# Values held back one step and taken in pairs: a two-layer transformer kernel on one core

## The reference

```
xn = layernorm(x)
x  = x + diff_attention(xn; 16 heads, two softmax maps each) + (fp6_quantised(xn) @ fp6_quantised(W).T + bias)
xn = layernorm(x)
x  = x + rope_attention(xn; 16 heads, one softmax map each) + mlp(xn; sign weights, 128 -> 512 -> 512 -> 128, relu)
```

## Time and profile before

| | us |
|---|---|
| median of 3 runs | 860.47 |
| the profiled execution: its own time | 859.55 |
| its span, first to last instruction | 857.8 |
| PE busy | 801.4 (93%) |
| ACT busy | 764.2 (89%) |
| DVE busy | 551.5 (64%) |
| POOL busy | 35.4 (4%) |

### The profile page before, as it was taken

The page is one execution under the profiler, slowest core; times in us unless marked ns, Lnnn a source line. Parts: engine busy times, 40 slices in busy tenths (PEclk is TensorE's granted clock), DMA queues, the critical chain, the costliest instruction groups (busy, mean ns, idle before and its releaser), DMA issues.

```text
span 857.8 us, 17781 instructions
## 1 busy us (share of the span) xinstructions
PE 801.4 (93%) x6735; PEld 283.6 (33%) x6735; DVE 551.5 (64%) x1216; ACT 764.2 (89%) x856; POOL 35.4 (4%) x56
## 2 busy tenths in 40 slices
...
GB/s 110 166 119 123 53 91 135 124 57 50 164 50 148 7 106 108 107 97 2 164 50 141 64 1 213 50 126 30 51 164 89 115 2 151 53 2 139 75 13 13
DMA packets 42114, 75.52 MB, mean 88 GB/s; under 512 B 5920, under 2 KB 7584, under 8 KB 42016
## 3 DMA queue, kind: packets, MB, share of 16 engines
...
HBM read 36.84 MB, written 35.65 MB: 85 GB/s over the span
## 4 chain that ended last, share of the span: by engine, by line
PE 70%; ACT 12%; DVE 9%; issue 5%; DMA 2%; SPq 1%; DVEq 0%; ACTq 0%
PE ps_pv L899 30%; PE ps_s L880 20%; ACT probs L726 12%; PE ps_misc L747 7%; PE ps_misc L751 7%; PE ps_misc L752 5%; PE ps_misc L740 2%; DMA q_ab<-shift 1%; DMA parts_dram<-qk_parts 1%; DVE pv_sb L1346 1%; DVE v_aug L1205 0%; DVE h_lo L1139 0%; ACT ff_out L676 0%; SPq L457 0%; DVE h_hi L1137 0%
## 5 line engine op out<-in xcount | busy, mean ns | idle before, releaser
L726 ACT ACTIVATE probs<-ps_s 128x1024 f32<-128x1024 f32 x768 | 725.8, 1048 | 54.8 <-PE ps_s L880 53.7
L899 PE MATMUL ps_pv<-probs,v_aug 128*32 128x512 f32 x3072 | 412.0, 608 | 8.6 <-ACT probs L726 4.6
L880 PE MATMUL ps_s<-q_ab,k_ab 18*128 18x512 f32 (+1 forms) x1088 | 142.6, 497 | 29.9 <-ACT probs L726 23.9
L880 PEld LDWEIGHTS ps_s<-q_ab,k_ab 18*128 18x128 f32 (+1 forms) x1088 | 54.6, 183 | 204.1 <-ACT probs L726 164.1
L899 PEld LDWEIGHTS ps_pv<-probs,v_aug 128*32 128x32 f32 x3072 | 61.7, 108 | 116.2 <-issue 82.8
L751 PE MATMUL ps_misc<-h_hi,k_w 128*128 128x512 f32 x192 | 85.8, 447 | 2.4 <-DVE v_aug L1205 1.2
L880 PE MATMUL ps_s<-q_c,k_c 34*128 34x512 f32 x448 | 84.1, 451 | 0.0
L1137 DVE CAST h_hi<-ff_out 128x512 fp32r<-128x512 f32 x64 | 27.4, 427 | 86.9 <-ACT ff_out L676 85.1
L1346 DVE STREAM_TRANSPOSE pv_sb<-ps_pv 128x512 f32<-128x512 f32 x48 | 34.4, 717 | 74.6 <-PE ps_pv L899 72.0
L752 PE MATMUL ps_misc<-h_lo,k_w 128*128 128x512 f32 x192 | 75.9, 395 | 0.0
L751 PEld LDWEIGHTS ps_misc<-h_hi,k_w 128*128 128x128 f32 x192 | 35.9, 187 | 88.9 <-issue 50.4
...
## 6 DMA issues: line engine op xcount, KB each, us to landing
...
parts_dram<-qk_parts SPq DMA_DIRECT2D x62, 256.0 KB, 4.0
...
x_all<-in_L_attn_x_dram POOLq DMA_DIRECT2D x7, 256.0 KB, 4.2
out_dram<-x_all POOLq DMA_DIRECT2D x7, 256.0 KB, 7.1
```

Source lines behind the costliest of these rows:

```text
L726: nc.scalar.activation(probs[:, U.slot(s), 2 * half:2 * half + 2], ps_s[:, 2 * pair:2 * pair + 2], ACT.Exp, scale=SCALE[U.layer]).then_inc ...
L880: ins = nc.tensor.matmul(ps_s[:, bank, :], k[row:row + n, slot, c * P:(c + 1) * P], q[row:row + n, slot, :], start=True, stop=True)
L899: ins = nc.tensor.matmul(ps_pv[32 * j:32 * j + 32, :], v_aug[:, U.v, c, a:a + 32], probs[:, U.slot(s), j, :], start=c == 0 and not odd, st ...
```

## The change

1. A step may be marked with an item `hold`. In a held step S, PE makes the scores and the jobs but not the values of S-2; in step S+1 the values of S-2 and S-1 come one behind the other, and then the jobs of S+1. The order of the values is worked out by `order_of_values`. A third number in a `hold` item has no effect.
2. `probs` has a fourth slot, so the exponentials of S wait for the values of S-4 only.
3. x is kept in a ring of four (`x_ring`), which makes room for the fourth slot. POOL loads sequences 2 and 3 where it loaded all, and sequence b+2 behind `x_t1` of b, once sequence b-2 is stored. The parked v goes to slot 0 of the ring.
4. The tables: 21 of the 48 steps of a turn of the loop are held, seven in each stage. Single steps are held in `FIRST` (2) and `LAST` (8). In `LOOP`, jobs move: `project1` and one half of `ff1` stay in A, three parts of `ff1` and `ff1_b` that were in A and the first steps of B are spread over B, and `quant_mm`, the last part of `ff1` and `ff1_b`, `ff2` and `ff2_b` come to stage C. `v1` moves from step 9 of A to step 8, and `qk_norm1` stays in step 9, but ahead of `take`. `exact0` moves from B to step 7 of C.

```diff
+RING = 4
+SLOTS = 4
@@
 LOOP = [
-    {0: [("ff0", -1, 0)], 1: [("take", -2, "C", 1), ("ff0", -1, 1)], 2: [("regroup", -2, "C", 1)], 3: [("q1", -1)],
+    {0: [("hold", 0, 0), ("ff0", -1, 0)], 1: [("take", -2, "C", 1), ("ff0", -1, 1)], 2: [("regroup", -2, "C", 1)],
...
-     7: [("rope", -1, "k", 0), ("rope", -1, "k", 1)], 9: [("v1", -1), ("take", 0, "A", 0), ("qk_norm1", -1)], 10: [("ff0", -1, 3)],
+     8: [("hold", 0, 8), ("v1", -1)], 9: [("qk_norm1", -1), ("take", 0, "A", 0)], 10: [("hold", 0, 10), ("ff0", -1, 3)],
...
+def order_of_values():
+
+    order, due = [], []
+    for S in range(STEPS * UNITS):
+        due += [S - 2] if S >= 2 else []
+        held = any(item[0] == "hold" for item in TABLE[S // STEPS].get(S % STEPS, []))
+
+        assert not held or (S % 8 != 1 and len(due) == 1), S
+        order.append([] if held else due)
+        due = due if held else []
+    return order, [*due, STEPS * UNITS - 2, STEPS * UNITS - 1]
@@
     def slot(self, s):
-        return (self.first_step + s) % 3
+        return (self.first_step + s) % SLOTS
@@
-        probs = sb("probs", [P, 3, 4, N], F32)
+        probs = sb("probs", [P, SLOTS, 4, N], F32)
@@
+            load_x(1, x1_loaded)
+            pool.wait_ge(scores_made, 2 * STEPS)
+            for b in range(2, RING):
+                load_x(b, x_loaded)
@@
+            def load_next(b):
+
+                if RING <= b < NSEQ:
+                    pool.wait_ge(stored, 16 * (b - RING + 1))
+                    load_x(b, x_loaded)
@@
-                        wait(act, pv_made, S - 2)
+                        wait(act, pv_made, S - SLOTS + 1)
@@
-                    if s >= 2:
-                        pv(U, s - 2)
-                    elif u > 0:
-                        pv(Unit(u - 1), STEPS - 2 + s)
+                    for earlier in order[STEPS * u + s]:
+                        pv(Unit(earlier // STEPS), earlier % STEPS)
                     run(items, holds)
```

More of the change, by code:

```diff
@@ L79 @@
      12: [("norm0", 1, 1), ("bias", 0), ("quant_mm", 0)], 14: [("norm0", 1, 2), ("norm0", 1, 3)], 15: [("norm0", 1, 4), ("x_t0", 1)]},
[L80 to L83, removed]
+    {0: [("q0", 1)], 1: [("take", 0, "A", 1)], 2: [("lambda", 0), ("regroup", 0, "A", 1)], 3: [("quant", 1, 0), ("v0", 1)],
+     4: [("quant", 1, 1), ("quant", 1, 2)], 5: [("k0", 1)], 6: [("quant", 1, 3)], 7: [("quant", 1, 4)], 9: [("exact0", 1)],
+     10: [("take", 0, "B", 0), ("regroup", 0, "B", 0)], 11: [("quant", 1, 5), ("quant", 1, 6)], 12: [("bias", 1)],
+     13: [("quant_mm", 1)]},
     {1: [("take", 0, "B", 1), ("regroup", 0, "B", 1), ("combine", 0, 0)], 3: [("combine", 0, 1), ("combine", 0, 2)],
@@ L103 @@
 LOOP = [
[7 rows of a table removed]
[L111 to L117, removed]
[7 rows of a table added]
+     3: [("quant", 1, 0)], 4: [("hold", 0, 20), ("ff1", -1, 1), ("quant", 1, 1)], 5: [("quant", 1, 2)],
+     6: [("hold", 0, 22), ("ff1_b", -1, 1)], 7: [("quant", 1, 3)], 8: [("hold", 0, 24), ("q0", 1)],
+     9: [("take", 0, "B", 0), ("quant", 1, 4)], 10: [("hold", 0, 26), ("ff1", -1, 2), ("quant", 1, 5)],
+     11: [("regroup", 0, "B", 0), ("quant", 1, 6)], 12: [("hold", 0, 28), ("ff1_b", -1, 2)], 13: [("bias", 1)], 14: [("k0", 1)]},
+    {0: [("hold", 0, 32), ("ff1", -1, 3)], 1: [("take", 0, "B", 1), ("regroup", 0, "B", 1), ("ff1_b", -1, 3)],
+     2: [("hold", 0, 34), ("quant_mm", 1), ("combine", 0, 0)], 3: [("combine", 0, 1), ("combine", 0, 2)],
+     4: [("combine", 0, 3), ("combine", 0, 4)], 5: [("combine", 0, 5)], 6: [("hold", 0, 38), ("v0", 1), ("out_t0", 0)],
[3 rows of a table added]
+     14: [("hold", 0, 46), ("ff_t", -1)]},
 ]
 LAST = [
[5 rows of a table removed]
[6 rows of a table added]
     {0: [("ff1", 5, 2), ("norm0", 7, 3)], 1: [("take", 6, "A", 1), ("norm0", 7, 4), ("ff1_b", 5, 2)],
@@ L128 @@
      4: [("q0", 7), ("quant", 7, 2), ("quant", 7, 3), ("quant", 7, 4), ("quant", 7, 5)], 6: [("ff1", 5, 3)],
-     7: [("ff1_b", 5, 3), ("k0", 7)], 8: [("bias", 7)], 10: [("quant", 7, 6)], 11: [("take", 6, "B", 0), ("regroup", 6, "B", 0)],
-     12: [("exact0", 7), ("v0", 7)], 14: [("ff2", 5)]},
-    {0: [("ff2_b", 5)], 1: [("take", 6, "B", 1)], 2: [("regroup", 6, "B", 1), ("v_move", 5), ("combine", 6, 0)],
+     7: [("ff1_b", 5, 3), ("k0", 7)], 8: [("bias", 7), ("hold", 0, 24)], 10: [("quant", 7, 6)],
+     11: [("take", 6, "B", 0), ("regroup", 6, "B", 0)], 12: [("exact0", 7), ("v0", 7)], 14: [("ff2", 5), ("hold", 0, 30)]},
+    {0: [("ff2_b", 5), ("hold", 0, 32)], 1: [("take", 6, "B", 1)], 2: [("regroup", 6, "B", 1), ("v_move", 5), ("combine", 6, 0)],
      3: [("combine", 6, 1), ("combine", 6, 2), ("ff_t", 5)], 4: [("combine", 6, 3), ("quant_mm", 7)],
@@ L1198, in job @@
                 elif name == "v1" and b in (5, 6):
-                    dve.wait_ge(stored, 16 * finished[0])
-                    taken(nc.vector.tensor_copy(x_all[:, b - 5].rearrange("p t d -> p (t d)"), ps))
+                    assert finished[0] == 5
+                    dve.wait_ge(stored, 16 * 5)
+                    wait(dve, v_moved, b - 5)
+                    taken(nc.vector.tensor_copy(waiting_values.rearrange("p t d -> p (t d)"), ps))
                 elif name in ("v0", "v1"):
```

46 lines of the change are left out of this document (24 added, 22 removed), and 36 rows, old and new, of tables (FIRST, LAST, LOOP).

## The result

The changed kernel takes 866.05 us (median of 13 runs, 862.2 to 869.16) against 860.45 of the kernel before (13 runs beside them, 858.54 to 864.66): a ratio of 1.0061, 95% interval 1.0044 to 1.0077. It is slower by 5.6 us, where I forecast 858.0, and lies outside the range of 850.5 to 865. Its profiled execution took 864.89, 5.3 more than that of before, so the two profiles can stand for the medians.

What follows compares the result with a forecast made beforehand. Whether PE brings ACT's scores in time bounds A and B; C is near both engines' limits. Loop -1.6, held steps outside -0.9 and +0.2 make -2.3: 859.55 becomes 857.2, median 858.1, written 858.0; range 850.5 to 865.

Steps and rivals of the forecast that it cites:

- A: First stage of a loop turn: PE's steps sum to 34.3 us against 36.8 before, -2.5.
- B: Second stage of a loop turn: PE's steps sum to 32.3 us against 34.6 before, -2.3.
- C: Third stage of a loop turn: jobs moved in are paid in full, 34.7 us against 30.3 before, +4.4.
- pairs: In A and B, a held step of 1.68 and the step behind it of 2.31 take 3.99 us.
- the second values: On PE, values directly behind values take 0.88 us, with bounds of 0.86 and 0.99.
- The wait for `take`: In step 11 of A, PE waits 0.8 us because take has gone behind the norm chain; bounds nothing to 1.5.
- Rival 1: C runs late: a DVE chain starting 1.5 us late delays PE, 6 over four turns, 864; chance 0.23.
- rival 4: Values behind values gain nothing on PE: a pair takes 4.10 us, 9 more over four turns, 867; chance 0.03.
- The first and last stages keep their order but for ten held steps: Outside the loop: about eight held steps save 0.11 us each, -0.9; first values held one step cost 0.2.
- -0.4 a turn, -1.6 over four: The loop: changes of -2.5, -2.3 and +4.4 us in A, B and C sum to this gain.
- The ring costs nothing: x loads: each lands in 4.2 us and is issued some 90 us ahead of the norm that reads it.
- project1 of b = 4 moves to step 6: Outside the loop: it comes four steps (8 us) ahead of the v that needs its store.

Runs made afterwards that it cites:

- e1: The changed kernel without its ten held steps outside the loop, those in the loop kept: 863.19 us, ratio 1.0045 to the kernel before.
- e2: The changed kernel with the loop's table of the kernel before, the ten held steps outside the loop kept: 865.18 us, ratio 1.0062 to the kernel before.
- e3: The changed kernel with no held step and the old loop table; ring, fourth slot and jobs moved outside the loop stay: 862.39 us, ratio 1.0036.
- f3: e1 with stage A rearranged (take before qk_norm1, ff0's last part a step later, step 4 not held): 860.04 us, ratio 0.9987 to the kernel before.
- f1: The changed kernel with useless identity transposes in PE's longest idle times outside the loop: 861.56 us, ratio 1.0008 to the kernel before.
- g2: The changed kernel without three held steps beside long waits (step 2 of stage 0, 14 of 18, 0 of 19): 865.3 us, ratio 1.006.

## Why the prediction was wrong

**What held.** A was 34.2 for 34.3, B 32.3 for 32.3, C 34.7 for 34.7. Held steps are 1.68 and pairs in B without a relu 3.97 to 4.01, for 3.99. PE in B, answering to the earlier trace rows, shows a held step with its half of `ff1` (333.76 to 335.44; the job starts 0.43 behind the scores) and the pair behind it (335.88 to 337.77, 1.89 where two separate values would take 1.98):

```profile
333.76 0.50 PE L918 MATMUL ps_s<-q_ab,k_ab 18*128 18x512 f32 x4
334.19 0.51 PE L789 MATMUL ps_misc<-h_hi,k_w 128*128 128x512 f32 x1
...
335.44 0.51 PE L918 MATMUL ps_s<-q_ab,k_ab 18*128 18x512 f32 x4
335.88 1.92 PE L937 MATMUL ps_pv<-probs,v_aug 128*32 128x512 f32 x16
337.77 0.51 PE L918 MATMUL ps_s<-q_ab,k_ab 18*128 18x512 f32 x4
```

So the second values cost 0.90 in this pair (1.89 less 0.99). In the pairs of C they come to 0.86 or 0.87 (395.00 to 396.86 is 1.86), the lower end of the range; I had taken 0.88. A job behind scores starts after 0.43 to 0.44 in A and B, as taken. C answers to the earlier trace rows; PE is busy 34.58 of its 34.73:

```profile
394.25 0.83 PE L918 MATMUL ps_s<-q_c,k_c 34*128 34x512 f32 x4
395.00 1.92 PE L937 MATMUL ps_pv<-probs,v_aug 128*32 128x512 f32 x16
396.86 0.73 PE L918 MATMUL ps_s<-q_c,k_c 34*128 34x512 f32 x4
```

The wait for `take` came where and as large as forecast: 0.8. PE and DVE in step 11 of A, answering to the earlier trace rows:

```profile
321.16 0.68 DVE L1247 TENSOR_REDUCE norm_max<-ps_misc 64x1 f32<-64x512 f32 x1 [0.80 <-PE ps_misc L836]
...
322.73 0.50 PE L918 MATMUL ps_s<-q_ab,k_ab 18*128 18x512 f32 x4
...
323.10 0.72 DVE L1385 STREAM_TRANSPOSE pv_sb<-ps_pv 128x512 f32<-128x512 f32 x1
...
323.96 1.92 PE L937 MATMUL ps_pv<-probs,v_aug 128*32 128x512 f32 x16 [0.73 <-DVE pv_sb L1385]
```

A second, 0.34 for the bank of `qk_norm1` in step 10, I had not listed; 34.2 took it in. The ring costs no wait by its loads, which land in 3.0. Rival 1 did not happen: C is 34.7 in each turn. Nor did rival 4: it needs 0.99 for values behind values, and they took 0.86 to 0.90. That the result lies near the 867 of rival 4 is a coincidence.

**What failed** is the step "The first and last stages keep their order but for ten held steps. About eight save 0.11 in the values, -0.9; and the first values, held one step in the first stage, cost 0.2." I had -0.7 there, and the square of e1, e2 and e3 measured +1.4 to +2.9 for the held steps. A saving of 0.11 a pair may be there, but some of those steps stand among long waits, and in stage 0 holding the values took work away from PE just when it had little: stage 0 is 37.6 to 39.6 in the four traces that hold its step 2 and 35.2 to 36.5 in the five that don't, all without fill. The sum had no term for the granted clock at all, although a row of the kernel before for stage 0 would have shown 0.87.

The same missing term is in "-0.4 a turn, -1.6 over four": an undisturbed turn gave 101.25 against 101.68, -0.4, but in the third turn of the profiled execution A took 1.6 more, and over the runs the new loop is not 1.6 faster but up to 0.9 slower. The wait of 0.8 for `take` was in the sum, and so was its place; what it lacked was that the sixteen matmuls behind it can run at half clock, as in 9 of 20 stages A. With f3's stage A, which shows no such drop, the four turns take 402.7, 4.5 less than before.

Another step failed too: "The ring costs nothing", with no term for the fourth slot or for the moved jobs. e3, which has these three and no held step, is 1.8 (median) to 3.1 (ratio) slower than the kernel before, and the interval of its ratio, 1.0016 to 1.0056, lies above 1. Which of the three it is stays open. "The first and last stages keep their order" is not true as it stands, since jobs move in stages 1, 17 and 21.

That filling idle time gives 4.5 back in the changed kernel and 2.9 in the one before, with a higher granted clock in both, is the direct evidence that the clock is a means by which idle time costs. It doesn't settle all: of the 5.6 between the two kernels the fill closes 1.7, and with both filled the change is still 3.9 behind (861.56 against 857.69). f1's profiled execution, its slowest at 864.25, shows where that can come from: its loop took 409.88, and three of its four stages A were at 35.6 to 36.1, with no fill in the loop. And the split of the ten held steps over places stays open, as g2 shows.

A smaller miss: "project1 of b = 4 moves to step 6, four steps (8 us) ahead of the v that needs its store" priced only the store. The move costs 1.1 in stage 17 through DVE, and a wait one stage later hides it. My reckoning from the profiled execution to the median, +0.9, was also unsafe: that execution had a granted clock of 0.989, above the kernel's average of 0.986.
